# Differential attention with two layer norms on one core: a shorter pause of the sums, a coarse mask inside the contraction, per-bank waits, and another order of the first loads

## The reference, cut to what matters

```
# x: (2, 1024, 128); 16 heads, each with two score maps of width d = 4: 32 maps per batch element
q = (x @ Wq).reshape(B, S, 32, 4).transpose(0, 2, 1, 3) * 4 ** -0.5
k = (x @ Wk).reshape(B, S, 32, 4).transpose(0, 2, 1, 3)
v = (x @ Wv).reshape(B, S, 16, 8).transpose(0, 2, 1, 3)
scores = jnp.where(causal_mask, -inf, einsum('bhqd,bhkd->bhqk', q, k))
probs = softmax(scores)                       # 64 maps of 1024 x 1024, fp32 accuracy
attn = (probs[map 0] - lam * probs[map 1]) @ v           # per head
attn = rmsnorm(attn) * rms_w * (1 - LAMBDA_INIT)
x = layernorm(x + concat(attn) @ Wo)
xr, xk = mu_r*x + (1-mu_r)*x_prev, mu_k*x + (1-mu_k)*x_prev
x = layernorm(x + sigmoid(xr @ W_r.T) * (square(relu(xk @ W_k.T)) @ W_v.T))
```

## Time and profile before

| | |
|---|---|
| three runs | 504.01, 507.17, 508.28 us; median 507.17 |
| profiled execution | 505.25 us, its span 503.5 us |
| busy | PE 418.9, DVE 391.2, ACT 354.7, POOL 198.2 us |
| max units, bursts | 288, 288 |
| stretches of the span | start 0 to 28.85, max units alone to 60.6, bursts to about 467, FFN and norms to 503.5 |

### The profile page before, as it was taken

One profiled execution on the slowest core, in us unless ns is written; L12 is line 12 of the kernel. 1 busy time (PEld: TensorE's weight loads), 2 busy tenths in 40 slices (PEclk: granted clock), 3 DMA queues, 4 the chain that ended last, 5 costly groups with the idle time before them and its releaser, 6 DMA issues.

```text
span 503.5 us, 14453 instructions
## 1 busy us (share of the span) xinstructions
PE 418.9 (83%) x5191; PEld 178.7 (35%) x5191; DVE 391.2 (78%) x504; ACT 354.7 (70%) x687; POOL 198.2 (39%) x349
## 2 busy tenths in 40 slices
PE   5665788898989898989898989889898978788682
PEld 3431323233434333333333333334242423344352
DVE  2769889797979999979797979898979894324633
ACT  3620168687878888968797969897969687756343
POOL 7000021253535364535354535545444445351512
PEclk9875569798979999979898979999989899989978
DMA  7695202011111120202020202020202010000001
GB/s 204 187 296 227 86 0 69 20 44 44 48 40 44 44 85 0 85 0 85 0 85 0 85 0 85 0 85 0 85 0 85 0 44 4 1 1 22 2 21 42
DMA packets 21082, 28.35 MB, mean 56 GB/s; under 512 B 3776, under 2 KB 8768, under 8 KB 21056
## 3 DMA queue, kind: packets, MB, share of 16 engines
q1 hardware_dynamic: 20624, 27.80, 17.5%
q10 hardware_dynamic: 432, 0.20, 0.2%
HBM read 18.29 MB, written 9.44 MB: 55 GB/s over the span
## 4 chain that ended last, share of the span: by engine, by line
PE 68%; ACT 15%; DVE 8%; issue 6%; DMA 1%; POOL 1%; ACTq 0%; POOLq 0%; DVEq 0%
PE acc L593 28%; PE ex L562 17%; ACT e_buf L898 11%; PE mx L516 7%; PE mx L508 6%; DVE part_max L989 5%; PE mx L690 1%; PE ex L624 1%; ACT o_tok L828 1%; PE ex L629 1%; PE mx L691 1%; DMA x_tok<-in_L_attn_x 1%; PE mx L675 1%; PE mx L710 1%; DVE rest L949 1%
## 5 line engine op out<-in xcount | busy, mean ns | idle before, releaser
L989 DVE TENSOR_REDUCE part_max<-mx 128x2 f32<-128x1024 f32 (+2 forms) x288 | 337.6, 1219 | 45.9 <-PE mx L508 35.8
L898 ACT ACTIVATE e_buf<-ex 128x512 f32<-128x512 f32 x576 | 312.1, 597 | 85.4 <-PE ex L562 81.0
L593 PE MATMUL acc<-e_buf,v_grp 128*32 128x256 f32 (+2 forms) x2200 | 185.5, 424 | 0.0
L562 PE MATMUL ex<-qe,ke 32*128 32x512 bf16 (+3 forms) x768 | 119.0, 346 | 44.0 <-ACT e_buf L898 29.2
L435 POOL TENSOR_SCALAR_AFFINE_SELECT e_buf<-e_buf 128x512 f32<-128x512 f32 x128 | 78.9, 634 | 169.5 <-ACT e_buf L898 169.4
L508 PE MATMUL mx<-km,qm 32*128 32x128 bf16 (+2 forms) x1280 | 124.4, 284 | 13.6 <-DVE part_max L989 12.1
L562 PEld LDWEIGHTS ex<-qe,ke 32*128 32x128 bf16 x768 | 30.9, 92 | 168.1 <-ACT e_buf L898 159.1
L593 PEld LDWEIGHTS acc<-e_buf,v_grp 128*32 128x32 f32 x2200 | 50.1, 115 | 65.6 <-issue 56.1
L508 PEld LDWEIGHTS mx<-km,qm 32*128 32x128 bf16 x1280 | 43.6, 96 | 25.9 <-DVE part_max L989 22.1
L516 PE MATMUL mx<-mask,pick 32*128 32x384 bf16 (+3 forms) x512 | 47.4, 308 | 0.0
L419 POOL TENSOR_TENSOR r_rms<-sq_eps,minus_half 128x16 f32<-128x16 f32 x15 | 43.7, 2910 | 1.2
(11 more groups left out here) (130 smaller groups left out, 266.3 us busy)
## 6 DMA issues: line engine op xcount, KB each, us to landing
qm<-q_rows SPq DMA_DIRECT2D x16, 256.0 KB, 2.7
km<-k_rows SPq DMA_DIRECT2D x16, 256.0 KB, 2.9
qe<-q_rows SPq DMA_DIRECT2D x16, 256.0 KB, 2.9
ke<-k_rows SPq DMA_DIRECT2D x16, 256.0 KB, 3.0
x_tok<-in_L_attn_x SPq DMA_DIRECT2D x2, 512.0 KB, 5.0
q_rows<-zero_rows SPq DMA_DIRECT2D x2, 512.0 KB, 5.8
k_rows<-ones_rows SPq DMA_DIRECT2D x2, 512.0 KB, 7.5
out<-v_all SPq DMA_DIRECT2D x4, 256.0 KB, 2.3
```

Source lines behind the costliest of these rows:

```text
L562: scored = pe.matmul(ex[:, ex_slot(b, i) % EX_BANKS, col:col + w], ke[par][rows, P * kb:P * (kb + 1)], qe[par][rows, q1 - w:q1], start=col ...
L593: last = pe.matmul(bank[STRIP * j:STRIP * (j + 1), hi - w:hi], v_grp[par][:, kb, j // 2, shift:shift + STRIP], e_buf[:, k % ESLOTS, j, col ...
L898: nc.scalar.activation(e_buf[:, k % ESLOTS, 2 * p + i, :], ex[:, ex_slot(b, i) % EX_BANKS, :], ACT.Exp).then_inc(s["exped"], 1)
L989: nc.vector.tensor_reduce(target, mx[m % 2][:].rearrange("p s (a b) -> p s a b", a=a), AX.X, ALU.max).then_inc(s["maxed"], 1)
```

## The change

1. **Terms and filling.** Row r of a strip is now term r // 4, dimension r % 4 (before: dimension r // 8). Rows 24 and 25 (FILL) take the maxima. Rows 26 to 28 hold a coarse causal mask: on the q side 1 where the 32-row chunk of the position within its block of 128 is 1, 2 or 3, on the k side -1e30 where the chunk of the key lies above. POOL builds eight such rows on eight partitions, SP stores them to DRAM (q_fill, k_fill) and fills both tensors from there. Masked units contract over 29 rows (ROWS), all others over 26 (COARSE).
2. **Mask matmuls.** They now cover only the 32 x 32 diagonal chunks: 4 x 32 columns each, all eight of a unit.
3. **Pause.** take_sums stands ahead of the exps of burst 4, turn and store in burst 7, INVERT_AT is 10. Burst 4 has no sum, burst 5 has halves 0 and 1, and from burst 6 on one half a burst.
4. **Waits.** score_pair waits for each bank just before the first matmul into it.
5. **Start.** write_parts issues one DMA for each term (12 instead of 6); for the first 32 rows SP issues the six of q, and ACT the six of k, after its last split copy of batch 0. The first loads of exp rows and of group 1 stand ahead of the other 96 rows.

The core of the diff: constants, write_parts and SP's start, then PE's max_unit and score_pair, then ACT's start and group.

```
+FILL = len(TERMS) * D
+COARSE = FILL + 2
+ROWS = COARSE + 3
-TAKE_AT, TURN_AT, MAXIMA_AT, INVERT_AT = 3, 5, 13, 8
+TAKE_AT, TURN_AT, MAXIMA_AT, INVERT_AT = 4, 7, 13, 10
-SUMS_AT |= {4: [], 5: [], 6: [(0, 0), (0, 1)], 7: [(0, 2), (0, 3)]}
+SUMS_AT |= {4: [], 5: [(0, 0), (0, 1)]}
...
+        def write_parts(eng, which, b, own, done):
+            subs = slice((b * P + own.start) // D, (b * P + own.stop) // D)
+            for part, need in ((0, "hi_done"), (1, "mid_done"), (2, "lo_done")):
+                eng.wait_ge(s[need], 4 * (b + 1))
+                for w in which:
+                    for i in (i for i, term in enumerate(TERMS) if term[w] == part):
+                        eng.dma_start((q_parts, k_parts)[w][subs, :, i, :], parts[w][part][own, b, :])\
+                            .then_inc(done, 16)
...
+            sp.wait_ge(s["fills_set"], 9)
+            for rows, fills in ((q_fill, q_fills), (k_fill, k_fills)):
+                sp.dma_start(rows, fills[:].rearrange("r b c t -> r (b c t)")).then_inc(s["fills_in"], 16)
...
+            sp.wait_ge(s["fills_in"], 32)
+            fill_rows(0, s["rows_head"])
+            write_parts(sp, (0,), 0, slice(0, HEAD), s["rows_head"])
+            sp.wait_ge(s["rows_head"], 16 * (2 + 2 * len(TERMS)))
             load_max_rows(sp, 0, 0)
-            write_parts(0, slice(HEAD, P), s["rows_b0"])
+            load_exp_rows(sp, 0, 0)
             load_max_rows(sp, 1, 1)
-            load_exp_rows(sp, 0, 0)
-            fill_rows(slice(P, 2 * P), s["rows_b1"])
-            write_parts(1, slice(0, P), s["rows_b1"])
+            write_parts(sp, (0, 1), 0, slice(HEAD, P), s["rows_b0"])
+            fill_rows(1, s["rows_b1"])
+            write_parts(sp, (0, 1), 1, slice(0, P), s["rows_b1"])
...
-                        rows = slice(STRIP * j, STRIP * (j + 1))
+                        rows = slice(STRIP * j, STRIP * j + used)
...
-                        cols = mask[rows, c, STRIP * c:P].unsqueeze(1).broadcast_to([STRIP, 4, P - STRIP * c])
+                        cols = mask[rows, c, own].unsqueeze(1).broadcast_to([STRIP, 4, STRIP])
...
-                for i in range(2):
-                    place_free(n, ex_slot(b, i))
-                parts_here = QUADS[b // 2]
-                for c, kb, col, w in parts_here:
+                for c, kb, col, w in QUADS[b // 2]:
                     q1 = BANK * (c + 1)
                     for i in range(2):
+                        if col == 0:
+                            place_free(n, ex_slot(b, i))
...
+                if b == 0:
+                    write_parts(act, (1,), 0, slice(0, HEAD), s["rows_head"])
...
+                    if b == TAKE_AT and not (static and n == 0):
+                        take_sums(n - 1, 1 - par)
                     if p == 0:
                         wait(act, s["summed"], NQ * n + k - ESLOTS + 1)
...
-                    if b == TAKE_AT and not (static and n == 0):
-                        take_sums(n - 1, 1 - par)
```

More of the change, by code:

```diff
@@ L499, in max_unit @@
                 matmuls, masked, _ = MAX_UNITS[m // 2]
+                used = ROWS if masked else COARSE
                 pair = 1 - m % 2
@@ L514, in max_unit @@
                         rows = slice(STRIP * j, STRIP * (j + 1))
[L515 to L516 removed]
+                        own = slice(STRIP * c, STRIP * (c + 1))
+                        cols = mask[rows, c, own].unsqueeze(1).broadcast_to([STRIP, 4, STRIP])
+                        last = pe.matmul(mx[m % 2][:, jj, :].rearrange("p (a t) -> p a t", a=4)[:, :, own],
                                          pick[rows, c, :], cols, start=False, stop=c == SUBS - 1,
```

65 lines of the change are left out of this document (34 added, 31 removed).

## The result

| kernel | median us (lowest to highest) | ratio to the kernel before, 95% interval |
|---|---|---|
| before | 507.73 (504.01 to 508.79, 4 runs) | 1 |
| the change | 490.72 (486.48 to 493.02, 4 runs) | 0.9668 (0.9585 to 0.9751) |

The change is faster by 3.3%, 17.0 us. 36 us were forecast (471.0, range 460 to 491): the direction was right, the gain less than half of what was forecast, and the time lies just inside the upper end of the range. The run that was profiled is the fastest of the four: 486.48 us, its span 484.7.

A forecast was written before the change was run, and what follows sets the result against it. No engine alone was taken as the bound; DVE's 21.7 us a group was the floor. From 505.25 us: +2.5 start, -2.2 cheaper masks, -1.5 group 0, -2 last groups, -31.0 for 14 intervals gave 471 us, range 460 to 491.

The forecast's parts named there:

- Group at full clock, 22.4 us: Each group's interval: DVE's 21.7 us plus 0.4 idle plus 0.3 for small things; ends 21.7 and 23.2.
- rival D: POOL late: the mask of burst 0 waits for the normalising chain, 0.5 to 1 us a group, 480 us; chance 0.08.
- The pause without sums halves, so I expect it to hold in most groups: Pause in each group: stretch without sums shrinks from 4.2 to about 2.1 us, so PE's clock holds in most groups.
- rival A: The clock still falls in most groups: 1.6 us a group in 10 to 12 groups, 489 us; chance 0.17.
- Start, +2.5 for ACT's six issues: Start: six DMA issues on ACT delay the copy of xT before the first max unit, +2.5 us; ends 1.8 and 3.6.
- Group 0, -1.5: Group 0, bursts 0 to 5: less waiting for both banks and a hole before burst 6, 1.5 us off.
- Masks 0.65 to 0.25 us: Masked bursts on PE: eight narrower mask matmuls take 0.25 us instead of 0.65, the burst 1.05 instead of 1.45.
- rival F: Matmul count, not columns, rules the masks: 0.50 us a unit, a masked burst 1.30, kernel 480 us; chance 0.03.
- One-bank waits, -2: Groups 14 and 15, some 20 bursts without a max unit: one wait a bank serves ACT sooner, 2 us off.
- B: Split waits add a gap between scores and unit each burst: 0.8 us more in 14 groups, 482 us; chance 0.10.
- C: Scores no longer run side by side: each burst gains 0.21 to 0.39 us, kernel 517 us at 0.25; chance 0.05.
- E: The pause only moves: DVE idles the old 1.5 us, the clock falls as before, 498 to 508 us; chance 0.05.

## Why the forecast was 20 us off

- **Group at full clock, 22.4 us: right in size, partly by luck.** 22.26 to 22.50. It came about differently. I had 0.4 us of DVE idle for the late unit 8 and 0.3 for small things; there is 1.0 (22.27 less 21.25), and 0.62 us of PE idle in each group goes to POOL's late mask. I had seen the moved chain end "next to its mask for the sums of burst 0" and counted it in the 0.3. Its own price, from the inversion put back, is 0.4 to 0.6 us a group, 6 to 8 us. So rival D, to which I gave 0.08, is true at its low end, and the 22.4 came out only because DVE's work is 21.25 and 21.45 us where I had kept 21.7 as a floor "that nothing in this change lowers". Why it is lower, no run shows.
- **"The pause without sums halves, so I expect it to hold in most groups": the step that failed.** The pause did halve; the clock fell in 5 and in 12 of 13 groups of the two profiles. At 1.3 and 1.5 us each this is 7 and 18 us: rival A, to which I gave 0.17, with a price (489 us) near the measured 490.72. The forecast had put the fallen clock at nothing. I argued from the length of the hole, and the row that speaks against it was already there: of the groups before, all with the same order, one kept its clock and another lost it. That said that something beside the length of the hole decides, and so gave no ground to be sure of the shorter one. The fill shows the cause: with 0.6 us more of matmuls in the pause and nothing else changed, every group holds, and the median is 471.56. That this is the forecast's number is partly luck: in its profile (475.04) the terms are start +2.7, group 0 +1.9, the 14 intervals -33.2 and the tail -1.6, where I had +0.3, -1.5, -31.0 and -2.0.
- **Start, +2.5 for ACT's six issues: mis-sized.** +4.5 at the first max unit, from 0.8 us an issue (the six take 4.83 us, where I had 3 for all with the gaps between them) and the half clock at which PE comes back (2.07 against 1.13 us). Undoing it gives back 4.1. Of the 2.2 us for cheaper masks 1.8 came: 4.5 later at the first unit is 2.7 later at the first copy. With the full masks put back 1.1 of them are lost again (33.36 to 58.82 us from unit to copy, against 33.32 to 57.72).
- **Group 0, -1.5: wrong in this profile, its cause open.** +1.9 in the first profile, at a granted clock of 0.50 to the end of the interval, where before it rose at 73 us. In the kernel with the filled pause it was 28.54; in the ten other profiles of kernels with the change it is 24.25 to 26.18 us, below before's 26.63, which is the forecast's sign. Four of these ten have the old doubled sums in group 0.
- **Masks 0.65 to 0.25 us: nearly right on PE, worth little at the end.** Eight take 0.31 us (195.88 to 196.19 between their start and the sums), and a masked burst is 1.13 us, not 1.05. For a sequencer with hardware decode off, the Trainium skill ("TensorE: Matmul & The Clock Gate", "Back-to-back issue gap") has 62 ns for a matmul, by which eight would take an estimated 0.50 us; the trace has 39 ns each, so rival F falls. How the decode was set here, no run shows. But with the full masks a group is 0.15 us longer and the kernel not slower. The long masked bursts were not what held the group up here.
- **One-bank waits, -2: not found.** The tail came out +1.8 in the first profile. The last of the 14 intervals shows a gain, 24.01 to 21.58 us, but there the clock had fallen before and held after. Behind it, in group 15's bursts 5 and 6 in the changed kernel, the clock falls again; PE and then ACT:

```profile
421.12 1.93 PE L616 MATMUL acc<-e_buf,v_grp 128*32 128x256 f32 x16
422.99 2.08 PE L713 MATMUL mx<-x1T,w_cur 128*128 128x512 f32 x2
```

```profile
427.23 1.08 ACT L925 ACTIVATE e_buf<-ex 128x512 f32<-128x512 f32 x2 [4.74 <-PE ex L585]
```

  The doubled sums take 1.93 us instead of the 1.07 of full clock, the FFN matmuls follow at the same pace ahead of the next scores, and ACT idles 4.74 us behind them. Where the fill holds the clock in both kernels, the last interval is 22.64 us before and 21.57 after, and the stretch behind it 75.6 and 75.9: about 1 us where 2 were forecast, and 0.8 of it every group has. With both waits back the total is 1 to 4 us higher, with ranges that overlap, so even the sign of the term is not shown.
- **Rivals B, C and E.** I had named more than 0.15 us between scores and unit as the sign of B and C. It is there: 0.24 to 0.27 us in several bursts, 0.38 in burst 8. But it costs nothing, since a plain burst is no longer than before and joining the waits again made no group shorter; B and C are refuted by that. Of E one half came true, as A: the clock still falls. The other half did not: the pause's holes went from three to one, and DVE's idle in a fast group from 1.5 to 1.0 us.

What stays open: why the clock in group 0 comes back between 70 and 80 us in ten profiles of kernels with the change and near 85 and 89 in two, even with the same instructions; what in the fill holds the clock, since no run varied its kind, length or place; and which of the masks, the split waits and the earlier take_sums brings the 0.8 us a group at full clock. Masks and split waits, undone one by one, cost no more than 0.15 us there. That each is covered by another is my guess; the earlier take_sums was never undone by itself.

## What to carry to other kernels

In this kernel a stretch of 2.2 us without sums, with PE busy for 2.18 us of the 3.00 around it, could cost the clock for some 3.5 us afterwards, and whether it did differed from group to group and from profile to profile with the same instructions. So count the slow groups in more than one profile before a gain is put down to an order of work. Then try the cheapest cure first, a few matmuls whose result is overwritten, in the hole itself; here one such line was worth more than a schedule worked out. And when a step is moved to close one hole, follow its chain to the last engine in it: here the inversion, moved two bursts, came out as a wait of the next group's first sums for POOL's masks, 0.5 us a group, and took back more than the 0.15 us that the shorter pause gave at full clock.

## What the runs showed of the hardware

- **Busy is not the same as clock.** PE's rows in group 0 of the change, two windows of 3 us from the middle and one from the end (columns as above):

```profile
72.00:75.00 3.00, 3.00 (x28) 0.54 (x22) 1.70 (x2) 1.65 (x4) 0.05 (x1) 0.50 0.00 0
...
84.00:87.00 3.00, 3.00 (x39) 1.19 (x31) 2.20 (x2) 1.67 (x4) 0.00 (x0) 0.50 0.02 5
87.00:90.00 3.00, 3.00 (x30) 0.67 (x26) 2.10 (x2) 2.04 (x4) 0.00 (x0) 0.68 0.40 109
```

  PE is busy in all of each window and has its low clock all the way from the first to the second; in between, one window of 3 us has 2.42 busy. In the profile with the inversion put back, where PE has the same sums to do, the clock had risen by 74, and in the second profile of this very kernel, whose windows from 72 to 81 are just as busy (3.00, 2.42 and 3.00 us), by 80.
- **The same program, other clocks.** The change lost the clock in 5 of 13 groups in one profile and in 12 of 13 in another; with the fill, in none of 13, and the runs of the old kernel with it lie within 2.8 us. The Trainium skill ("TensorE: Matmul & The Clock Gate", "Part 1: The HAM clock gate") says of a kernel's first matmuls that how many run at the low clock differs between runs of one kernel. This case agrees: of the first projection's pairs of matmuls, two start at the slow pace in the first profile (2.06 and 1.77 us) and three in the second (2.07, 1.91 and 1.44), before the pairs take 1.02. The windows give a granted clock of 1.00 there, so it is the pace alone that tells. It shows the same in the middle of a kernel, by the counts above.
- **A DMA issue is work for the engine that issues it.** Six from ACT took 4.83 us while SP issued six in 4.32, 0.7 to 0.8 us each; alone, at the start, ACT's first took 0.45 and 0.61. On ACT a copy and the projection behind it waited for that; with all twelve on SP the first unit came 4.1 us earlier.
